# The beginning of an adaLN attention kernel: a semaphore for each load, column blocks, and a moved mask table

## What is computed

```python
base  = einsum('bsi,oi->bso', x, weight) + bias           # wc, b_cond
low   = einsum('bsi,bri->bsr', x, a_sel)                  # la, chosen by the adapter's number
y     = base + scale * einsum('bsr,bor->bso', low, b_sel) # lb
qkv   = einsum('bsh,oh->bso', y, w_qkv) + b_qkv           # wq
...                                                       # rotary, causal softmax, context, w_dense
x1    = x + attention(y)
# second attention: keys of the cache count where position < cache_seqlens[b]
valid_c = arange(L)[None, :] < cache_seqlens[:, None]     # becomes mask_row
```

## Time and profile before

| | us |
|---|---|
| median of 3 runs (1418.09 to 1422.16) | 1420.65 |
| the profiled execution's own time | 1419.12 |
| its span | 1417.3 |
| TensorE busy | 1356.8 (96%) |
| TensorE weight loads busy | 1141.4 (81%) |
| VectorE busy | 1092.3 (77%) |
| ScalarE busy | 860.1 (61%) |
| GpSimd busy | 655.3 (46%) |

### The profile page before, as it was taken

How to read it: one execution, slowest core, us unless ns; L and a number is a source line. 1 busy time by engine, 2 the same in 40 slices (tenths; PEclk the granted TensorE clock), 3 DMA queues, 4 the chain that set the end, 5 groups by cost and what they waited for, 6 DMA issues and landing times.

```text
span 1417.3 us, 26026 instructions
## 1 busy us (share of the span) xinstructions
PE 1356.8 (96%) x7832; PEld 1141.4 (81%) x7832; DVE 1092.3 (77%) x2968; ACT 860.1 (61%) x2499; POOL 655.3 (46%) x652
## 2 busy tenths in 40 slices
PE   4999998679999999999999999999999999999988
PEld 3655665368888888888888888888888888888877
DVE  3787787458888888888888888887888888888855
ACT  1556666446666666667666766676666666666631
POOL 1344554445365446545453635364436544554511
PEclk9999999899999999999999999999999999999999
DMA  7444444442212222121213121212131221212121
GB/s 259 143 148 150 145 148 156 129 118 47 75 31 60 46 75 54 37 75 31 60 36 84 32 60 31 75 31 61 32 85 41 54 75 31 61 30 65 31 75 60
DMA packets 193518, 107.56 MB, mean 76 GB/s; under 512 B 140897, under 2 KB 178274, under 8 KB 191970
## 3 DMA queue, kind: packets, MB, share of 16 engines
q1 hardware_dynamic: 192224, 105.38, 28.0%
q10 hardware_dynamic: 1154, 0.50, 0.1%
HBM read 101.66 MB, written 37.75 MB: 98 GB/s over the span
## 4 chain that ended last, share of the span: by engine, by line
PE 77%; DVE 2%; ACT 1%; issue 0%; POOL 0%; DVEq 0%; ACTq 0%; POOLq 0%
PE b_ps L1072 11%; PE b_ps L1074 11%; PE b_ps L1073 11%; PE b_ps L1121 10%; PE b_ps L1142 5%; PE b_ps L1136 5%; PE b_ps L1135 5%; PE b_ps L1153 4%; PE b_ps L1152 4%; PE b_ps L1159 4%; PE b_ps L1097 2%; PE b_ps L796 1%; PE b_ps L795 1%; PE b_ps L794 1%; PE b_ps L1102 0%
## 5 line engine op out<-in xcount | busy, mean ns | idle before, releaser
L1265 ACT ACTIVATE b_pf<-b_sm,b_nb,b_rstd 128x640 f32<-128x640 f32 x256 | 235.0, 918 | 103.4 <-DVE b_nb L1370 103.1
L1271 ACT ACTIVATE b_p_h<-b_ps 128x640 fp32r<-128x640 f32 x256 | 180.3, 704 | 178.6 <-PE b_ps L1121 178.0
L1384 DVE TENSOR_TENSOR b_p_l<-b_ps,b_p_h 128x640 fp32r<-128x640 f32 x256 | 210.5, 822 | 77.7 <-ACT b_p_h L1271 69.8
L1363 DVE CUSTOM_DVE_ANT_0 b_sm<-b_ps,mask_row 128x640 f32<-128x640 f32 x256 | 208.9, 816 | 2.0 <-PE b_ps L1074 1.7
L1121 PE MATMUL b_ps<-ident,b_pf 128*128 128x128 f32 x1280 | 181.6, 273 | 7.8 <-DVE b_p_l L1384 5.2
L1072 PE MATMUL b_ps<-w_h,x1t_h 128*128 128x512 f32 (+1 forms) x512 | 179.4, 350 | 7.7 <-POOL w_l L1452 6.3
L1379 DVE TENSOR_SCALAR b_pf<-b_pf,b_ri 128x640 f32<-128x640 f32 x256 | 159.7, 624 | 27.7 <-DVE b_ri L1376 0.5
L1072 PE MATMUL b_ps<-b_kt_h,b_qt_h 128*128 128x320 f32 x512 | 174.1, 340 | 2.0 <-DVE b_mx L1363 1.2
L1074 PE MATMUL b_ps<-w_h,x1t_l 128*128 128x512 f32 (+1 forms) x512 | 173.9, 340 | 0.0
L1121 PEld LDWEIGHTS b_ps<-ident,b_pf 128*128 128x128 f32 x1280 | 151.7, 140 | 27.1 <-issue 6.8
L1073 PE MATMUL b_ps<-w_l,x1t_h 128*128 128x512 f32 (+1 forms) x512 | 173.4, 339 | 0.0
(11 more groups left out here) (163 smaller groups left out, 3296.8 us busy)
## 6 DMA issues: line engine op xcount, KB each, us to landing
kv_of_batch<-in_kv SPq DMA_DIRECT2D x128, 256.0 KB
b_ck<-kv_of_batch SPq DMA_DIRECT2D x64, 256.0 KB, 3.7
b_cv<-kv_of_batch SPq DMA_DIRECT2D x256, 64.0 KB, 2.2
raw<-in_w SPq DMA_DIRECT2D x32, 384.0 KB, 5.1
raw<-in_wo SPq DMA_DIRECT2D x32, 256.0 KB, 3.6
a_xt<-in_xt SPq DMA_DIRECT2D x8, 256.0 KB, 4.9
a_xin<-in_x SPq DMA_DIRECT2D x8, 256.0 KB, 5.6
x<-a_x SPq DMA_DIRECT2D x8, 256.0 KB, 5.2
```

Of the source, the lines that this page charges most:

```text
L1265: act.activation(pf[:, h % 2], sm[:, h % 2], ACT.Exp, bias=nb[:, m.b % 2, h:h + 1], scale=rstd[:, m.b % 4, h:h + 1], accum_out=rs[:, m.b % ...
L1271: act.activation(p_h[:, :, h * P:(h + 1) * P], turned_row, ACT.Copy).then_inc(ph_sb, 1)
L1363: dve.tensor_tensor_reduce(sm[:, h % 2], score_row, mask_row[:, m.b], 1.0, MASKED, ALU.add, ALU.max, mx[:, k, h:h + 1]).then_inc(mx_sb, 1)
L1384: dve.tensor_tensor(p_l[:, :, cols], turned_row, p_h[:, :, cols], ALU.subtract).then_inc(pl_sb, 1)
```

## The change

- la, lb and b_cond, and each of four blocks of 128 columns of wc, get a semaphore of their own; SP issues la, lb, the four blocks, b_cond. `low_rank(0)` waits for la, `cond(0)` for lb and before each output block for that block of wc, `y_out(0)` for b_cond.
- wq is loaded in two parts, the q columns (1 MB) ahead of b_qkv, cos, sin and ident under `qkv_in`, the k/v columns (512 KB) behind them under `kv_in`, for which `project_kv(0)` waits.
- key_row moves from ScalarE's loads to SP's queue, between the k/v columns and the rest, with its own semaphore.
- ScalarE issues the choice's loads first, waits for GpSimd's memset of vz, copies 32 columns of it into a scrap tile (the first activation of the program), and then issues pages and the loads of `tables`.
- The masks leave `table_angles`. `table_masks` makes those of batches 0 to 3 in slot -1 between `kv_out(0)` and `rope_sum(0)`, and those of 4 to 7 in slot 0 behind `table_products`.

```diff
@@ -126,13 +126,16 @@
         nb = sb("nb", [P, H1])
         rs = sb("rs", [P, H1])
         ri = sb("ri", [P, H1])
+        scrap = sb("scrap", [P, 2 * D1])
         pr = sb("pr", [P, 4, 4, P])
         pt = sb("pt", [P, 8, 4, P])
         cxt = sb("cxt", [P, KT, P])
         xb = sb("xb", [P, 2, D])
         x1 = sb("x1", [P, 2, D])
 
-        cond_in, qkv_in, rest_in, ids_in = sem("cond_in"), sem("qkv_in"), sem("rest_in"), sem("ids_in")
+        la_in, lb_in, b_cond_in, kv_in = sem("la_in"), sem("lb_in"), sem("b_cond_in"), sem("kv_in")
+        wc_in = [sem(f"wc_in{o}") for o in range(KT)]
+        qkv_in, rest_in, ids_in = sem("qkv_in"), sem("rest_in"), sem("ids_in")
         adapters_in, id_sb, chosen_sb = sem("adapters_in"), sem("id_sb"), sem("chosen_sb")
         xt_in, xin_in = sem("xt_in"), sem("xin_in")
         low_ps, low_sb, yt_ps, yt_sb = sem("low_ps"), sem("low_sb"), sem("yt_ps"), sem("yt_sb")
@@ -155,11 +158,11 @@
             return 0 <= b < B
 
         block = ctx.enter_context(nc.Block())
-        cond_weights = ((la, "la"), (wc, "wc"), (lb, "lb"), (b_cond, "b_cond"))
         choice = ((adapters, "adapters"), (ls, "ls"), (which, "which"))
-        qkv_weights = ((wq, "wq"), (b_qkv, "b_qkv"), (cos, "cos"), (sin, "sin"), (ident, "ident"))
+        qkv_small = ((b_qkv, "b_qkv"), (cos, "cos"), (sin, "sin"), (ident, "ident"))
+        QKV_LOADS = 1 + len(qkv_small)
         rest = ((blocks, "blocks"), (causal, "causal"), (wd, "wd"), (b_dense, "b_dense"))
-        load_tables, table_angles, table_products, table_sines = tables(nc, ctx, t, consts)
+        load_tables, load_key_row, table_angles, table_masks, table_products, table_sines = tables(nc, ctx, t, consts)
 
         @block.sync
         def _(sp):
@@ -177,9 +180,19 @@
                 sp.dma_start(x1_dram[bass.ds(b, 1)].rearrange("b s d -> (b s) d"), x1[:, b % 2]).then_inc(x1_out, 16)
 
             load(0)
-            for part, signal in ((cond_weights, cond_in), (qkv_weights, qkv_in), (rest, rest_in)):
-                for dst, name in part:
-                    sp.dma_start(dst[:], t[name]).then_inc(signal, 16)
+            sp.dma_start(la[:], t["la"]).then_inc(la_in, 16)
+            sp.dma_start(lb[:], t["lb"]).then_inc(lb_in, 16)
+            for o in range(KT):
+                cols = slice(o * P, (o + 1) * P)
+                sp.dma_start(wc[:, :, cols], t["wc"][:, :, cols]).then_inc(wc_in[o], 16)
+            sp.dma_start(b_cond[:], t["b_cond"]).then_inc(b_cond_in, 16)
+            sp.dma_start(wq[:, :, 0:D], t["wq"][:, :, 0:D]).then_inc(qkv_in, 16)
+            for dst, name in qkv_small:
+                sp.dma_start(dst[:], t[name]).then_inc(qkv_in, 16)
+            sp.dma_start(wq[:, :, D:], t["wq"][:, :, D:]).then_inc(kv_in, 16)
+            load_key_row(sp)
+            for dst, name in rest:
+                sp.dma_start(dst[:], t[name]).then_inc(rest_in, 16)
             for c in range(KT):
                 sp.dma_start(raw[:, c], t["w2"][0, c]).then_inc(raw_in[c], 16)
             sp.wait_ge(ids_in, 16)
@@ -205,7 +218,7 @@
             def low_rank(a):
 
                 if a == 0:
-                    pe.wait_ge(cond_in, 16 * len(cond_weights))
+                    pe.wait_ge(la_in, 16)
                 pe.wait_ge(xt_in, 16 * (a + 1))
                 wait(pe, xl_sb, a - 2)
                 for k in range(KT):
@@ -216,7 +229,11 @@
 
                 pe.wait_ge(low_sb, a + 1)
                 wait(pe, qt_sb, a)
+                if a == 0:
+                    pe.wait_ge(lb_in, 16)
                 for o in range(KT):
+                    if a == 0:
+                        pe.wait_ge(wc_in[o], 16)
                     for k in range(KT):
                         pe.matmul(ps[:, M1, o * P:(o + 1) * P], wc[:, k, o * P:(o + 1) * P], xt[:, k],
                                   start=k == 0, stop=False)
@@ -226,7 +243,7 @@
             def project_q(a):
 
                 if a == 0:
-                    pe.wait_ge(qkv_in, 16 * len(qkv_weights))
+                    pe.wait_ge(qkv_in, 16 * QKV_LOADS)
                 pe.wait_ge(yt_sb, a + 1)
                 wait(pe, bd_sb, KT * a)
                 for k in range(KT):
@@ -235,6 +252,8 @@
 
             def project_kv(a):
 
+                if a == 0:
+                    pe.wait_ge(kv_in, 16)
                 pe.wait_ge(yt_sb, a + 1)
                 for k in range(KT):
                     mm = pe.matmul(ps[:, M1, 0:QKV1 - D], yt[:, k], wq[:, k, D:], start=k == 0, stop=k == KT - 1)
@@ -361,7 +380,7 @@
 
             def y_out(a):
                 if a == 0:
-                    act.wait_ge(cond_in, 16 * len(cond_weights))
+                    act.wait_ge(b_cond_in, 16)
                 act.wait_ge(yt_ps, a + 1)
                 wait(act, kv_ps, a)
                 wait(act, q_ps, a)
@@ -429,9 +448,11 @@
                 if inside(b):
                     probs_out(b, 5)
 
-            act.dma_start(pages[:], t["pages"]).then_inc(ids_in, 16)
             for dst, name in choice:
                 act.dma_start(dst[:], t[name]).then_inc(adapters_in, 16)
+            act.wait_ge(zero_sb, 1)
+            act.activation(scrap[:], vz[:, 0].rearrange("p t d -> p (t d)"), ACT.Copy)
+            act.dma_start(pages[:], t["pages"]).then_inc(ids_in, 16)
             load_tables(act)
             slots(slot)
 
@@ -452,7 +473,7 @@
 
             def q_out(a):
                 if a == 0:
-                    dve.wait_ge(qkv_in, 16 * len(qkv_weights))
+                    dve.wait_ge(qkv_in, 16 * QKV_LOADS)
                 dve.wait_ge(q_ps, a + 1)
                 wait(dve, rope_ab, a)
                 wait(dve, v_sb, a)
@@ -527,6 +548,8 @@
                     invert(b, 3)
                 if inside(b + 1):
                     kv_out(b + 1)
+                if b == -1:
+                    table_masks(dve, range(4))
                 if inside(b):
                     mask(b, 5)
                     mask(b, 6)
@@ -549,6 +572,7 @@
                     probs_out(b, 4)
                 if b == 0:
                     table_products(dve)
+                    table_masks(dve, range(4, B))
                 if inside(b + 1):
                     mask(b + 1, 0)
                 if inside(b):
@@ -612,7 +636,7 @@
 
             pool.memset(vz[:], 0.0).then_inc(zero_sb, 1)
             pool.wait_ge(zero_sb, 1)
-            pool.wait_ge(qkv_in, 16 * len(qkv_weights))
+            pool.wait_ge(qkv_in, 16 * QKV_LOADS)
             slots(slot)
 
 
@@ -637,12 +661,15 @@
     half_sine = sb("half_sine", [P, B, HD // 2])
     minus_sine = sb("minus_sine", [P, B, HD // 2])
     cosine = sb("cosine", [P, B, HD // 2])
-    loaded, step, sines = sem("loaded"), sem("step"), sem("sines")
-    loads = ((lens, "lens"), (token, "token"), (inv, "inv"), (norms, "norms"), (key_row, "key_row"))
+    loaded, step, sines, key_row_in = sem("loaded"), sem("step"), sem("sines"), sem("key_row_in")
+    loads = ((lens, "lens"), (token, "token"), (inv, "inv"), (norms, "norms"))
 
     def load_tables(act):
         for dst, name in loads:
             act.dma_start(dst[:], t[name]).then_inc(loaded, 16)
+
+    def load_key_row(sp):
+        sp.dma_start(key_row[:], t["key_row"]).then_inc(key_row_in, 16)
 
     done = [0]
 
@@ -665,7 +692,11 @@
         for part in TWO_PI:
             then(dve, dve.scalar_tensor_tensor(out=angle[:], in0=turns[:], scalar=-part, in1=angle[:], op0=ALU.mult, op1=ALU.add))
         then(dve, dve.tensor_scalar(angle[:], angle[:], 3.1415925, -3.1415925, ALU.min, ALU.max))
-        for b in range(B):
+
+    def table_masks(dve, batches):
+
+        dve.wait_ge(key_row_in, 16)
+        for b in batches:
             dve.tensor_scalar(mask_row[:, b], key_row[:], lenf[:, b:b + 1], MASKED, ALU.is_ge, ALU.mult)
 
     def table_products(dve):
@@ -688,7 +719,7 @@
         act.activation(sine[:], angle[:], ACT.Sin).then_inc(sines, 1)
         act.activation(half_sine[:], angle[:], ACT.Sin, scale=0.5).then_inc(sines, 1)
 
-    return load_tables, table_angles, table_products, table_sines
+    return load_tables, load_key_row, table_angles, table_masks, table_products, table_sines
 
 
 def phase2_consts(nc, ctx):
```

## The result

The changed kernel takes 1416.55 us in the median of 7 runs (1415.14 to 1417.62), the kernel before 1419.92 in 7 runs beside it: ratio 0.9975, 95% interval 0.9965 to 0.9985. That is 3.4 us less, a real gain that stays just inside the 0.3% which I had called hard to tell from nothing. The forecast was 1416.3, a gain of 4.3. The profiled execution took 1415.53 us with a span of 1413.7.

What follows compares the result with a forecast made beforehand. TensorE was taken to bound part one, except at its beginning and in the batch with the rotary tables. A gain of 6.2 us minus 1.9 gave 4.3, so 1420.65 falls to 1416.3 us, range 1413.0 to 1421.0.

Steps and rivals of the forecast that it cites:

- The first product: Beginning of part one: TensorE's first product starts at la's landing, 5.55 us instead of 10.75.
- The second product: Beginning of part one: TensorE's second product starts near 8.4 us instead of 14.63, 6.2 us earlier.
- The length of the second product: Beginning of part one: stays 6.5 us, about two slow and two fast blocks, 1.0 us either way with the clock.
- The later loads: Loads behind the column blocks: ident lands at 16.2, norms at 15.5 to 16.5, key_row by 20.7; no cost.
- My rival of slow split loads: Beginning: split loads keep the early 175 GB/s and land late; 1418.9 us with half that delay; chance 0.25.
- Rival 3: Before rope_sum: key_row landing after 23.6 us holds VectorE, each us late costing one, 1425 at 32.2; chance 0.07.
- Masks, first half: Before rope_sum: four masks, 1.9 us, fit where VectorE idled 3.36 us while GpSimd multiplied; cost nothing.
- Masks, second half: Batch 0, behind the table products: four masks put their full 1.9 us on the path, bounds 0 to 2.9.
- rival 1: Batch 0: the masks are hidden or the clock is kinder; gain 6.2 us, time 1414.4; chance 0.18.
- SP's queue: Part one: SP's five more issues, 2.3 us, are not the bound, as it waits 3.8 us for the last x1.
- The sum: Part one: 6.2 us gained at the beginning minus 1.9 in batch 0 gives 4.3, carried to the barrier.
- Rival 4: Beginning: the first copy still waits, for the choice or a second table load; gain 1.8 us, 1418.8; chance 0.08.

Runs made afterwards that it cites:

- no_scrap: The changed kernel without the scrap copy and its wait, so the function table loads when the low-rank result is ready; 1418.79 us in one run.
- after_again: The changed kernel itself, unedited, measured once more on the chip that also ran three variants; 1416.41 us, ratio 0.9978 to the kernel before.
- one_wc: The changed kernel with wc as one load of 1 MB instead of four column blocks; 1416.88 us in one run.
- masks_early: The changed kernel with all 8 masks between the table angles and the q copy; 1413.0 us, ratio 0.9956 to the kernel before.
- sem_only: The kernel before with one edit, a semaphore each for la, wc, lb and b_cond; 1417.47 us, ratio 0.9974 to the kernel before.
- both: The changed kernel with all 8 masks early and 12 pages a slot; 1412.4 us, ratio 0.9954 to the kernel before.
- early12: The changed kernel with 12 pages instead of 13 gathered per slot of part one; 1416.39 us, ratio 0.998 to the kernel before.

## Why the prediction held, and where its steps were off

*The first product* was mis-sized by 0.5 us: la landed at 6.0, not 5.5. The two executions with the old order of the loads on both queues have it in at 5.5 and 5.35, the ten with the new order at 5.9 to 6.7. So the new order costs the first product about 0.5 us, at least 0.4; which of its parts does is open.

*The second product* came at 8.68 for a forecast of 8.4, all of it from the first one. The choice was ready at 6.7, and `which` no longer mattered; the first block was in time. The table load was worth its 1.28 us and no drain, as no_scrap shows.

*The length of the second product* I kept at 6.5 us. Counted up to the bias copy it was 6.58 in the kernel before and 7.48 in the changed one, since TensorE's pace doubled only in the third block, and 6.43 in after_again. That is the one block either way that the text allowed, and the profiled execution had the slow side of it. Together: 5.05 us at q, and 6.1 in after_again, for a forecast of 6.2.

*The later loads* all landed in time, mostly sooner than forecast. My rival of slow split loads fell:

```profile
a_wc<-in_wc SPq DMA_DIRECT2D x4, 256.0 KB, 6.2
a_wq<-in_wq SPq DMA_DIRECT2D x1, 1024.0 KB, 7.1
...
t_key_row<-in_key_row SPq DMA_DIRECT2D x1, 320.0 KB, 7.6
...
t_norms<-in_norms ACTq DMA_DIRECT2D x1, 128.0 KB, 5.8
ident<-in_ident SPq DMA_DIRECT2D x1, 64.0 KB, 6.8
```

ident landed at 9.11 + 6.8 = 15.9 (16.2 forecast, of which I gave 1 us to the 512-byte rows of the blocks; with wc whole, in one_wc, it landed at 15.2, so the blocks cost 0.7, and whether by their rows or by their later issue is not separated), norms at 9.9 (15.5 to 16.5 forecast), key_row at 17.8. Norms had been behind the 1.5 MB of wq; now it is issued at 4.13 and wq at 6.81. So the angles were done at 14.7, and VectorE idled 6.5 us before the q copy: the place that masks_early uses, which I did not see because I had put the angles' end at 20.3. Rival 3, key_row holding VectorE, did not occur: it landed 5.4 us before it was needed.

*Masks, first half: this step failed.* I costed them at nothing, for the cover of GpSimd's rope. They cost 0.87 us, since cover on the timeline is not cover when both engines share a read path: the masks took 4.40 us beside rope instead of 1.93, and rope 3.78 instead of 3.14. The trace before had it in an instruction that I did not look up, the second half of rope_sum:

```profile
L468 DVE TENSOR_TENSOR a_kr<-a_rope_a,a_rope_b x8: 686/1522/1524, 32.3 to 232.5; 128x512 f32<-128x512 f32 x8
```

Its shortest is 0.69 us, in slot -1 with GpSimd idle; its median, beside GpSimd's normalizing, 1.52.

*Masks, second half.* 1.9 us on the path, of the range 0 to 2.9: the pause grew by 1.84, and the first turned probabilities came 1.9 us later behind rope_sum on the mean of six executions against four. The upper bound of 2.9 was for a longer stretch at the lower clock, and a part of it is there: 0.6 us on average. Here reading what stood behind VectorE's queue was right, and rival 1 fell.

*SP's queue* I called no bound, on its 3.8 us wait. It is nearly one: in the changed kernel, masks_early, one_wc and sem_only it waited 2.4 to 4.5 us for landings, more than the 1.7 or 1.8 of the rest. The late x1 of the kernel before was itself a slow dense layer, so the slack I read there was of one execution. It changed no number, because x1 and the gathers both moved by 3 us or more.

*The sum.* At the xt mark the gain was 3.0 us in the profile; the medians say 3.4 and, on another chip, 3.0 (0.9975, 0.9978). My 4.3 was 6.2 - 1.9. In the profiled execution it went 5.05 at q, less 0.9 up to rope_sum, less 1.9 up to the end of the pause, and 0.7 back in the stretch behind it, which took 30.4 us in the kernel before and 29.6 in the changed one. Both executions ran a part of it at the lower clock; 0.5 of the 0.7 is TensorE's wait for VectorE's maxima (0.49 us at 77.24 before), which the changed execution, slow in the matmuls ahead of that place, does not have. So the gain came out 0.9 to 1.3 us short of the forecast: 0.87 of it is the shared read path, the step that I had wrong. In this pair the later second product adds 0.3 and one slow block 0.9, which after_again does not have, and that stretch of batch 0 takes 0.7 off again. Two things on the time are luck. The 0.7 us given back hide a part of the loss in this pair of profiles. And the median of the changed kernel lies within 0.3 us of the forecast 1416.3 only because the kernel before came out 0.7 us lower in 7 runs than in the 3 that I had started from; the gain is the fairer test. Rival 4 did not occur.

## What to carry to other kernels

A group semaphore costs the landing of its last member; splitting it can be as much as a whole rearrangement (0.9974 alone here, 0.9975 for all), and what is moved aside has to be put where its engine is idle, not only where the timeline shows a pause: masks_early, the same change with all masks before the q copy, doubles it to 0.9956 (1413.0 us), and with 12 pages a slot it measured 0.9954 (1412.4 us). Before an instruction of VectorE is costed at nothing beside GpSimd, look how long instructions with the same operands take in the trace with GpSimd busy and idle. And after every move, forecast each load's landing anew: a small load in front of a large one lands several us sooner, and that opens places.

## What the runs showed of the hardware

- VectorE and GpSimd: four masks beside rope took 4.40 us instead of 1.93, with two SBUF inputs 5.73 instead of 3.27, and with one SBUF and one PSUM input no longer than alone. In the first two cases the whole comes within 0.7 us of one after the other: 4.40 against 1.93 + 3.14 = 5.07, and 5.73 against 3.27 + 3.14 = 6.41.
- The same code (changed and after_again), with products one and two at the same 0.01 us, had its q products at 17.45 and at 16.39, and its last dense layer took 3.70 and 5.58 us. For the kernel before, the windows view of that layer shows a mean granted clock of 0.65, for the changed one 1.00 (length, busy us by engine, clock, DMA share, GB/s):

```profile
266.92:272.59 5.67, 5.67 (x8) 2.23 (x8) 0.00 (x0) 0.00 (x0) 0.00 (x0) 0.65 0.45 136
```

```profile
263.08:266.78 3.70, 3.70 (x8) 1.43 (x8) 0.00 (x0) 0.00 (x0) 0.00 (x0) 1.00 0.43 133
```

- The function table was loaded while ScalarE still waited for the choice (sem_only, 7.51, the copy at 10.63). There a table load behind one wait and ahead of another was free. With nothing to wait for it cost its 1.28 us and no more (no_scrap).
- In batch 0 the way from the first turned probabilities to the xt mark took 29.2 us at a mean granted clock of 1.00 (both, sem_only), 29.6 at 0.95 (changed, one_wc) and 31.2 at 0.90 (early12), for the same instructions.
